# An LSTM with a feed-forward network behind it: seven block products over the last 32 steps instead of 24

## The reference

```python
def step(carry, xw_t):
    prev_h, prev_c = carry
    a = xw_t + prev_h @ Wh
    i, f, o = sigmoid(a[:, :Hd]), sigmoid(a[:, Hd:2*Hd]), sigmoid(a[:, 2*Hd:3*Hd])
    g = tanh(a[:, 3*Hd:])
    next_c = f * prev_c + i * g
    next_h = o * tanh(next_c)

h = concatenate([hs, -hs], axis=-1)
h = relu(s0 * (h @ sign(k0))) * 2      # 512 (256 by symmetry) -> 1024
h = relu(s1 * (h @ sign(k1))) * 2      # 1024 -> 1024
y = x + s2 * (h @ sign(k2))            # 1024 -> 256
```

## Time and profile before

| | us |
|---|---|
| median of three runs (272.89 to 273.32) | 272.96 |
| the profiled execution | 273.06 |
| its span (first to last instruction) | 271.2 |
| PE busy (matmul) | 267.2 |
| PE loading weights | 219.9 |
| DVE busy | 215.4 |
| ACT busy | 174.6 |
| POOL busy | 48.1 |

### The profile page before, as it was taken

The page is one execution under the profiler, slowest core; times in us unless marked ns, Lnnn a source line. Parts: engine busy times, 40 slices in busy tenths (PEclk is TensorE's granted clock), DMA queues, the critical chain, the costliest instruction groups (busy, mean ns, idle before and its releaser), DMA issues.

```text
span 271.2 us, 8903 instructions
## 1 busy us (share of the span) xinstructions
PE 267.2 (99%) x3568; PEld 219.9 (81%) x3568; DVE 215.4 (79%) x769; ACT 174.6 (64%) x522; POOL 48.1 (18%) x70
## 2 busy tenths in 40 slices
PE   8999999999999999999999999999999999999995
PEld 6888888878999999999998899998887676666563
DVE  3878888888888888888888888887777777997355
ACT  4789786878566667655765576556777867733320
POOL 0010000012211112331222102000222225603030
PEclk9999999999999999999999999999999999999999
DMA  7980000000000000000010001000000010100003
GB/s 210 346 342 1 4 2 0 2 4 2 2 0 4 4 2 22 22 2 5 2 42 0 2 4 41 2 2 4 4 0 2 2 42 0 41 0 0 2 0 116
DMA packets 5432, 8.72 MB, mean 32 GB/s; under 512 B 656, under 2 KB 3472, under 8 KB 5264
## 3 DMA queue, kind: packets, MB, share of 16 engines
q1 hardware_dynamic: 5104, 7.64, 8.1%
q10 hardware_dynamic: 288, 0.52, 0.5%
HBM read 6.07 MB, written 2.10 MB: 30 GB/s over the span
## 4 chain that ended last, share of the span: by engine, by line
PE 98%; DVE 1%; POOL 0%; issue 0%; POOLq 0%
PE WK L555 36%; PE WK L538 14%; PE G L517 11%; PE WK L573 10%; PE G L508 10%; PE ACC L587 6%; PE G L573 4%; PE WK L604 2%; PE ACC L604 1%; PE G L649 1%; PE G L538 1%; PE ACC L538 1%; DVE x L886 1%; PE G L555 0%; POOL zero L1094 0%
## 5 line engine op out<-in xcount | busy, mean ns | idle before, releaser
L555 PE MATMUL WK<-h,k 128*128 128x256 f16 (+1 forms) x856 | 107.7, 276 | 0.0
L555 PEld LDWEIGHTS WK<-h,k 128*128 128x128 fp8e5 x856 | 80.8, 98 | 11.3 <-issue 0.2
L814 ACT ACTIVATE tT<-aT 128x128 f32<-128x128 f32 x126 | 39.0, 310 | 44.6 <-DVE aT L1033 43.4
L1033 DVE TENSOR_REDUCE aT<-G 128x128 f32<-128x256 f32 x128 | 48.2, 418 | 7.7 <-PE G L517 6.3
L701 ACT ACTIVATE G<-xw 128x256 f32<-128x256 f32 x126 | 46.6, 370 | 0.0
L538 PE MATMUL WK<-xs,wxs 128*128 128x512 f32 x168 | 42.5, 400 | 0.0
L517 PE MATMUL G<-h,w 128*128 128x64 f16 x1008 | 39.5, 192 | 0.0
L508 PEld LDWEIGHTS G<-h,w 128*128 128x128 f16 x1008 | 32.9, 96 | 6.7 <-DVE h L1050 5.1
L538 PEld LDWEIGHTS WK<-xs,wxs 128*128 128x128 f32 x168 | 30.4, 188 | 5.9
L508 PE MATMUL G<-h,w 128*128 128x32 f16 x1008 | 35.2, 177 | 0.0
L517 PEld LDWEIGHTS G<-h,w 128*128 128x128 f16 x1008 | 33.2, 97 | 0.0
(11 more groups left out here) (116 smaller groups left out, 283.9 us busy)
## 6 DMA issues: line engine op xcount, KB each, us to landing
x<-in_x SPq DMA_DIRECT2D x3, 512.0 KB, 8.4
out_y<-x SPq DMA_DIRECT2D x10, 128.0 KB, 1.8
xw<-in_wh SPq DMA_DIRECT2D x4, 256.0 KB, 5.0
k<-in_k SPq DMA_DIRECT2D x1, 1024.0 KB, 10.2
out_y<-x SPq DMA_DIRECT2D x4, 192.0 KB, 1.9
x<-in_x ACTq DMA_DIRECT2D x2, 256.0 KB, 3.6
xw<-in_wx SPq DMA_DIRECT2D x4, 128.0 KB, 4.0
xw<-in_wx SPq DMA_DIRECT2D x2, 256.0 KB, 5.2
```

Of the source, the lines that this page charges most:

```text
L555: ins = eng.matmul(layer_src(tile), w, rhs, start=a == 0, stop=last)
L814: eng.activation(tT[:, B * j0:B * j1], aT[:, j0:j1].rearrange("p j b -> p (j b)"), ACT.Tanh, scale=half_gain0 if t == 0 else half_gain).th ...
L1033: eng.tensor_reduce(aT[:, j0:j1], G[g][:, 0:256].rearrange("p (j h b) -> p j b h", h=2, b=B), op=ALU.add, axis=AX.X).then_inc(added[g])
```

## The change

The steps are cut in four portions of 8 and two of 16, so that N1 is portion 4 (steps 32 to 47) and N2 portion 5 (steps 48 to 63); the seven products have 512 columns instead of 384, and portion 3 (steps 24 to 31) is the last with a plain layer 2. `fill` is 2.06 in all steps from 1 on. Layer 1 of N1 is spread over later places of portion 3's layer 2, its last two tiles between the p1 products. The output products k = 0 to 3 of portion 3 follow p1 tiles 0 and 1 in the loop; the tail keeps k = 4 to 7. The planner's guesses for the eviction of N1 and the emptying of N2's tiles grow. Since the wider terms need more room, the buffers xs and wxs are given up after use for t23 and tq01, and the terms' high parts wait for the last x matmul or for p2 or its like before they overwrite.

```diff
-CHUNKS = ((0, 8), (8, 8), (16, 8), (24, 8), (32, 8), (40, 12), (52, 12))
-N1, N2 = 5, 6
+CHUNKS = ((0, 8), (8, 8), (16, 8), (24, 8), (32, 16), (48, 16))
+N1, N2 = 4, 5
...
-    return 3.4 if t < 0 else 1.8 if t < 1 else 2.3 if t < 9 else 2.2 if t < 16 else 2.3
+    return 3.4 if t < 0 else 1.8 if t < 1 else 2.06
...
-    return 0.48 if tile[0] == "y" else 0.67 if tile[0] == "x" else 0.95 if tile[:2] == (0, N1) else 0.38
+    return 0.48 if tile[0] == "y" else 0.67 if tile[0] == "x" else 1.3 if tile[:2] == (0, N1) else 0.38 if tile[0] in (0, 1) else 0.67
...
-    return {"mix": 0.65, "y": 0.74, 0: 0.93}[chore[0]]
+    return {"mix": 0.65, "y": 0.74, 0: 1.25}[chore[0]]
...
-        at = (2, 2, 3, 4, 5, 6, 6, 7) if c == 0 else (0, 1, 2, 3, 4, 5, 6, 6) if c < N1 - 1 else (1, 2, 3, 4, 5, 6, 6, 7)
-        return [((0, c + 1, n), 4) for n in range(8) if at[n] == m]
+        at = (2, 2, 3, 4, 5, 6, 6, 7) if c == 0 else (0, 1, 2, 3, 4, 5, 6, 6) if c < N1 - 1 else (3, 4, 5, 6, 7, 7)
+        return [((0, c + 1, n), 4) for n in range(len(at)) if at[n] == m]
...
-    return order + [((f"p{q}", m), 8) for q, m in ((1, 0), (1, 1), (1, 2), (2, 0), (1, 3), (2, 1), (2, 2), (2, 3))]
+    for tile in (("p1", 0), (0, N1, 6), ("p1", 1), (0, N1, 7), ("p1", 2), ("p2", 0), ("p1", 3), ("p2", 1), ("p2", 2), ("p2", 3)):
+        order.append((tile, matmuls(tile)))
+        if tile[0] == "p1" and tile[1] < 2:
+            order += [(("o", N1 - 1, 2 * tile[1] + k), 4) for k in range(2)]
+    return order
...
-    others = outs(N1 - 1, *range(8))
+    others = outs(N1 - 1, *range(4, 8))
...
-                empty_at[tile] = 1.6 + 2.2 * (tile[2] % 4) + (1.7 if tile[2] < 4 else 3.4)
+                empty_at[tile] = 1.6 + 2.8 * (tile[2] % 4) + (2.1 if tile[2] < 4 else 4.2)
...
-        xs = sb("xs", [P, 2, 2, 2, 512], F32R)
-        wxs = sb("wxs", [P, 2, 2, NJ, 128], F32R)
+        with nc.sbuf_tensor("xs", [P, 2, 2, 2, 512], F32R) as xs, nc.sbuf_tensor("wxs", [P, 2, 2, NJ, 128], F32R) as wxs:
+            pass
+        t23 = sb("t23", [P, 2, 4, NW], F32)
+        tq01 = sb("tq01", [P, 2, 4, 2, NW], F16)
...
-                e.wait_ge(seeded[1], 32)
+                e.wait_ge(seeded[1], 40)
                 eng.activation(p1s[:, tile[1]], layer_src(tile), ACT.Copy).then_inc(p1_made)
...
             def term_hi(i, k):
                 e.wait_ge(t_made[i], k + 1)
-                eng.activation(tq[:, i, k, 0], term(i, k), ACT.Copy).then_inc(t_hi[i])
+                if i < 2:
+                    e.wait_ge(x_mm, 4 * NJ)
+                elif i == 3:
+                    e.wait_ge(prod_mm[2], 4)
+                eng.activation(tq[i][:, k, 0], term(i, k), ACT.Copy).then_inc(t_hi[i])
```

More of the change, by code:

```diff
@@ L322, in lstm_ffn @@
         seven = sb("seven", [P, 1], U32)
-        h1 = sb("h1", [P, 2, 16 * NW], F16)
+        h1 = sb("h1", [P, 2, 16 * B * CHUNKS[0][1]], F16)
         h2 = sb("h2", [P, 8, 2, NW], F16)
@@ L362, in lstm_ffn @@
         r12 = cut(xflat, 20 * NW, 2, NW)
-        tq = cut(xflat[:, 22 * NW:38 * NW].bitcast(F16), 0, 4, 4, 2, NW)
-        b22 = cut(xflat[:, 38 * NW:42 * NW].bitcast(F16), 0, 4, 2, NW)
+        b22 = cut(xflat[:, 22 * NW:26 * NW].bitcast(F16), 0, 4, 2, NW)
+        tq = [tq01[:, 0], tq01[:, 1], cut(xflat[:, 26 * NW:30 * NW].bitcast(F16), 0, 4, 2, NW), b1[:, 0:4]]
         t4f = cut(w16[:, :].rearrange("p a j k c -> p (a j k c)").bitcast(F32), 0, 4, NW)
@@ L367, in lstm_ffn @@
         qs, d5 = r1[:, 0:4], r12
-        c11, c12 = cut(h1[:, 0], 0, 4, 2, NW), cut(h1[:, 0], 8 * NW, 4, 2, NW)
-        t23 = cut(h1[:, 1].bitcast(F32), 0, 2, 4, NW)
+        c11, c12 = cut(h1[:, 0], 0, 4, 2, NW), cut(h1[:, 1], 0, 4, 2, NW)
         c12f, c22f, c21f = t1f, t23[:, 0], t23[:, 1]
@@ L434, in out_sum @@
             return TILE[bank["y", mo]] if c == N2 else ACC[mo]
-        factors = {1: (a11, b1[:, 0:4]), 2: (a12, b1[:, 4:8]), 3: (mix[:, 3], b22), 4: (a22, tq[:, 3]),
-                   5: (mix[:, 0], tq[:, 0]), 6: (mix[:, 1], tq[:, 1]), 7: (mix[:, 2], tq[:, 2])}
+        factors = {1: (a11, b1[:, 0:4]), 2: (a12, b1[:, 4:8]), 3: (mix[:, 3], b22), 4: (a22, tq[3]),
+                   5: (mix[:, 0], tq[0]), 6: (mix[:, 1], tq[1]), 7: (mix[:, 2], tq[2])}
         out_parts = {N1: (11, c11, 21, c21), N2: (12, c12, 22, c22)}
@@ L908, in term_lo @@
                 e.wait_ge(t_hi[i], k + 1)
-                eng.tensor_tensor(tq[:, i, k, 1], term(i, k), tq[:, i, k, 0], ALU.subtract).then_inc(t_lo[i])
+                eng.tensor_tensor(tq[i][:, k, 1], term(i, k), tq[i][:, k, 0], ALU.subtract).then_inc(t_lo[i])
             def q_sum(m):
```

## The result

The changed kernel takes 280.95 us (median, 280.89 to 281.24), the kernel before on the same chip 273.14: 1.028 times as long (95% interval 1.026 to 1.031). The forecast was 281.6 in a range of 277.8 to 286.0. The profiled execution took 281.24 us with a span of 279.4.

A forecast was written before the change was run, and what follows sets the result against it. The prediction took the recurrence's floor of 3.065 us a step, not PE, to bound the changed loop. Start 22.0, loop 194.0, tail 63.8 and 1.8 outside the span gave 281.6 us, range 277.8 to 286.0.

The forecast's parts named there:

- Rival (1): The loop follows PE's budget: steps of 2.94 to 2.98 us, time 271.1 us, 0.7% faster; chance 0.05.
- rival (4): In loop and tail, evictions thin out so steps stay at the floor and pairs hide: 276.7 us; chance 0.04.
- Removed work: Loop: 13.9 us of PE work leave it, but the floor of 3.065 us a step limits the gain to 8.1.
- On top of the floor: Loop: delays of DVE and ACT add 3.9 us, between 1.5 and 7, making the loop 194 us.
- (a): Loop steps with two DVE evictions: later reductions, 0.09 us each in 19 steps, 1.7 us in all.
- (b): Steps 1 to 8: long DVE operations delay reductions, 0.14 us on two steps, 0.02 on six, 0.4 in all.
- (c): Steps behind an x_hi: tanh waits for two x evictions on ACT, 0.25 us on two steps, 0.5 in all.
- (d): Steps 48 to 63: longer ACT and DVE evictions at 512 columns, with PE's coarser grain, 1.3 us in all.
- The tail: After the start of step 63: matmuls +12.1 us, y_add wait +0.3, last addition and transfer +0.3, 63.8 in all.
- Rival (2): Wide matmuls, in loop and tail, take 0.131 us instead of 0.216, giving 260 us; chance 0.01.
- POOL: Loop: r1_rest grows from 0.92 to about 1.2 us, costing nothing unless p2 products reach it within a step.
- Rival (3): Larger collisions: ACT and DVE hold up 10 more steps, with 2 us at the pairs, 286.5 us; chance 0.10.

The follow-up runs named there:

- e2: The changed kernel with 7 of the 16 matmuls of each plain layer-2 tile left out (24 us of PE work): 281.12 us.
- e3: The changed kernel with DVE's low-part evictions of the 64 plain tiles shrunk to one column, products using the high part twice: 279.29 us.
- e1: The kernel before with 7 of the 16 matmuls of each plain layer-2 tile left out (some 30 us of PE work): 270.4 us.
- e9: The changed kernel with layer 1 tile 5 of portion 4 moved behind the first p1 tile: 281.03 us.
- e7: The changed kernel with DVE's y addition of portion 3 one pair earlier: 280.94 us.
- e4: The changed kernel with the output products k = 0 to 3 of portion 3 back in the tail: 284.45 us.
- e6: The changed kernel with four portions of 9 steps and two of 14, fill 2.19, p1's tile 3 ahead of p2: 275.47 us.

## Why the prediction was right, step by step

**What bounds the kernel.** Right. The floor, read from a few lightly loaded steps of the kernel before, held in the kernel after and all its variants: no step from 1 on is shorter than 3.06 us, whatever is taken from PE (e2) or from DVE (e3). Rival (1), with its steps of 2.94 to 2.98, is out, and so is rival (4): the evictions did not thin out and the tail came to 63.4 us, not 62.9.

**Removed work.** "A gain of 8.1 us and not of 13.9" is borne out by e1 and e2: the first part of what leaves PE shortens the loop, the rest doesn't. The fillers are 19 in a step such as 21, whose fillers all have 256 columns, as the planner's sum said.

**On top of the floor.** The sum was 3.9 us, measured 193.65 - 190.0 = 3.65. That the two lie so close is in part luck: (a) was too small, (b), (c) and (d) were too large, and two delays had no term at all. The terms, each step's length less 3.065:
(a) Two evictions: 10 steps at 3.13, 11 at 3.17 to 3.19, and one of 3.37 (step 16) with three DVE operations of 0.42 us in it: 2.2 us, not 1.7. I counted 19 steps where there are 22, at 0.09 each. The first kind costs 0.06; in the second the first of the two evictions starts 0.30 and not 0.26 after the step does, when ACT's high part ends, and the step costs 0.11. e3 brought 2.0 of it back.
(b) Long DVE operations: steps 8 and 9, 0.26 together (0.4 forecast); in step 9 the reductions start 0.98 after the step does, 0.99 forecast.
(c) ACT at the start: steps 2 and 4, 0.24 together, where 0.25 each was forecast: the term was twice too large. That tanh waits behind the evictions is right, and by about the time that I read: in step 4 it starts 0.71 us after the reductions do, 0.26 more than the usual 0.45. What I left out is what step 56 shows as well: a tanh that starts late takes 0.51 us where it takes 0.64 otherwise.
(d) Wide evictions: step 56 +0.38, step 61 +0.26: 0.6 us, half of the 1.3 forecast. The ACT operation, bounded by 0.48 and 0.68, is 0.58 to 0.60. e9 shows the first of these causes; that step 61 waits for ACT's c11_hi is read from the trace and was not tried.
Without a term: step 53 +0.24, unexplained (below), and step 15 +0.08, where h is done and PE starts 0.15 us later instead of 0.05, behind six x matmuls (1.64 us); read from the trace, not tried.

**The tail.** The chain after, in order of time (start us, us, what):

```profile
238.12 13.81 PE WK L578 x64
```

That is 0.2158 us a matmul, taken as 0.2167. With the small terms the forecast was +12.7 us, and it came out as +12.3: 256 x 0.2158 + 1.7 - 45.1 = 11.9 for the matmuls, 0.1 for the stall and 0.3 at the end, where the span now outlasts PE by 3.3 us and before by 3.0. (Two slips in the prediction, neither of which enters the forecast: the upper bound of +14.2 should have read +14.4, and the wide matmuls that it counts as 320 are 352, 96 in the loop and 256 in the tail.) The pairs' DVE operations take 0.69 us each, 0.61 start to start, as forecast; a pair takes 2.67 and 2.60 us, 2.5 forecast:

```profile
221.79 0.69 DVE L909 SCALAR_TENSOR_TENSOR t1f<-WK,xw 128x512 f32<-128x512 f32 x1 [0.91 <-ACT xw L760]
...
224.46 0.69 DVE L909 SCALAR_TENSOR_TENSOR t1f<-WK,xw 128x512 f32<-128x512 f32 x1
...
227.06 0.86 DVE L895 SCALAR_TENSOR_TENSOR x<-ACC,sc,x 128x256 f32<-128x256 f32 x2
227.84 0.68 DVE L909 SCALAR_TENSOR_TENSOR t1f<-G,xw 128x512 f32<-128x512 f32 x1
```

The stall of the outputs behind y_add is there, in its place, with 0.11 us for 0.3 (e7). Rival (2) is out: 0.131 us a matmul is nowhere in the wide stretches. The figure behind it, 131 ns for sustained pairs of weight load and matmul of 512 columns, is from the Trainium skill (TensorE: Matmul & The Clock Gate, Back-to-back issue gap); the pairs here do not reach it. The isolated gap that the same section of the Trainium skill gives, columns at 2.4 GHz plus 2.5 ns, makes 215.8 ns, an estimate from that page, and the row above has just that, in a stretch of 64.

**POOL.** r1_rest took 1.16 us (1.2 forecast) and cost nothing in the change as made. e4 shows the price of the condition: 1.4 us in one step. The prediction had named the condition and not how near it was.

**Rival (3)**, larger collisions, had its mechanism in the steps of (a) and (d), but far fewer of them.

What stays open: step 53 after is 0.24 us too long because h's DVE operation starts that much later after tanh of c than in other steps (0.46 us of wait instead of 0.22). The kernel before has the same at step 52 (3.39 us), and so has every variant but e6. I found no operation that explains it. Being in both kernels it is hardly part of the difference between them, but it is part of what lies above the floor.

## What to carry to other kernels

Where a serial chain runs beside filling work, find the steps in which the filling ran out: their length is the floor, and what is taken from the busy engine pays only down to it. Work moved from behind such a chain into it is free as long as the chain is at its floor, and the same move is paid in the loop where the filler sets the pace (the 16 output matmuls: -1.9 us in one kernel; +0.8 in the other, 1.5 of it in the loop). Before widening a tile at a border between such a stretch and one in which the engine is never idle, multiply out the second: here the tail took 12.3 us for the 4.5 that the loop could give.

## What the hardware showed that was not expected

- Idle time of the weight port is not idle time of PE. 0.42 + 0.28 us of waiting before the loads of L609 cost 0.11 us.
- PE's queue holds fillers and recurrence in one order: a filler that waits for POOL (0.71 us at the port in e4) and the 14 wide matmuls behind it kept a ready h waiting from 210.1 to 211.51.
- A DVE eviction of one column still took 0.16 us (e3), against 0.42 for 256 columns and 0.69 for 512 (L886 after): some 0.15 us and 1.04 ns a column. Two of one column took 0.44 us of DVE's time in a step, and the step was no longer for it (3.06 to 3.07 us).
- A late tanh is not paid in full: 0.26 us late cost 0.12 (step 4), 0.51 late cost 0.38 (step 56), because its two operations then take 0.51 to 0.52 us instead of 0.64.
